# Moving a weight's mean-of-magnitudes pass ahead of the small-weight preparation in a fused layer on eight cores

## What is computed

```python
def _L0_attn_ref(x, Wa, ba, Wb, bb, Wout, bout):
    a = jnp.tanh(jnp.einsum('btd,sd->bts', x, Wa) + ba)
    b = jnp.tanh(jnp.einsum('btd,sd->bts', x, Wb) + bb)
    ...                      # scan over t: h = a_t * h + b_t, hs = all h
    return x + jnp.einsum('bts,ds->btd', hs, Wout) + bout

def _L0_ffn_ref(x, weight, bias):
    scale = jnp.mean(jnp.abs(weight))
    w_t = jnp.clip(jnp.round(weight / (scale + EPS)), -1.0, 1.0)
    w_ste = weight + jax.lax.stop_gradient(w_t * scale - weight)
    return jnp.einsum('bsi,oi->bso', x, w_ste) + bias

xn = _layernorm(x, axis=-1)
x = x + _L0_attn_ref(xn, ...) + _L0_ffn_ref(xn, ...)
```

## Time and profile before

| | us |
|---|---|
| median of 3 runs | 740.21 (740.07 to 740.62) |
| the profiled execution's own time | 739.39 |
| its span, slowest core (core 5) | 737.8 |
| fastest core (core 3) | 732.8 |
| PE busy | 590.1 (80% of the span) |
| DVE busy | 348.9 (47%) |
| ACT busy | 235.6 (32%) |
| POOL busy | 216.9 (29%) |

### The profile page before, as it was taken

One profiled execution on the slowest core, in us unless ns is written; L12 is line 12 of the kernel. 1 busy time (PEld: TensorE's weight loads), 2 busy tenths in 40 slices (PEclk: granted clock), 3 DMA queues, 4 the chain that ended last, 5 costly groups with the idle time before them and its releaser, 6 DMA issues.

```text
span 737.8 us, 11310 instructions; the slowest of 8 cores (732.8 to 737.8 us)
## 1 busy us (share of the span) xinstructions
PE 590.1 (80%) x3804; PEld 312.0 (42%) x3804; DVE 348.9 (47%) x303; ACT 235.6 (32%) x250; POOL 216.9 (29%) x742
## 2 busy tenths in 40 slices
PE   0121244425999999999999999999999999999995
PEld 0021234423444444454444444444444454454442
DVE  0000099983245564545555544445555545555521
ACT  1275434533223222223322223322222223322220
POOL 1000022354233333333334333333333333333310
PEclk9999999999999999999999999999999999999998
DMA  8979557801234333333333334333333333333322
GB/s 227 281 258 331 188 166 260 290 26 58 66 114 158 119 118 114 115 115 115 115 115 115 115 123 139 132 141 138 127 116 114 115 115 115 115 115 115 115 85 87
DMA packets 17071, 103.02 MB, mean 140 GB/s; under 512 B 4566, under 2 KB 4598, under 8 KB 4598
## 3 DMA queue, kind: packets, MB, share of 16 engines
q1 hardware_dynamic: 9590, 51.96, 22.2%
q0 software_dynamic: 7424, 50.34, 17.9%
HBM read 68.73 MB, written 33.55 MB: 139 GB/s over the span
## 4 chain that ended last, share of the span: by engine, by line
PE 66%; DMA 8%; ACT 8%; DVEq 4%; ACTq 4%; DVE 3%; issue 3%; SPq 2%; POOLq 1%; POOL 0%
PE pffn L513 15%; PE pffn L516 15%; PE pffn L528 15%; PE pffn L524 15%; ACT xnT L297 4%; DMA vv<-wf 4%; ACTq L296 3%; PE pab L501 3%; DVE wbn L345 2%; PE ptr L538 2%; DMA wasb<-wb 2%; DVEq L344 2%; SPq L171 2%; ACT xnT L293 1%; ACT xnT L232 1%
## 5 line engine op out<-in xcount | busy, mean ns | idle before, releaser
L513 PE MATMUL pffn<-w_rhs,xnT 128*128 128x512 bf16 x512 | 194.8, 380 | 0.0
L516 PE MATMUL pffn<-w_rhs,xnT 128*128 128x512 bf16 x512 | 194.6, 380 | 0.0
L524 PE MATMUL pffn<-w_rhs,xnT 128*128 128x512 bf16 x512 | 194.0, 379 | 0.0
L528 PE MATMUL pffn<-w_rhs,xnT 128*128 128x512 bf16 x512 | 194.0, 379 | 0.0
L357 DVE TENSOR_REDUCE sums<-sx 128x1 f32<-128x2048 f32 x32 | 73.1, 2286 | 148.7 <-DMA sx<-x 148.0
L293 ACT COPY xnT<-ptr 128x1024 bf16<-128x1024 bf16 x31 | 31.4, 1012 | 243.3 <-PE ptr L538 243.3
L275 ACT ACTIVATE xnb<-sx,nmr,yr 128x2048 bf16<-128x2048 f32 x31 | 64.9, 2094 | 102.2 <-POOLq L621 102.1
L391 DVE SCALAR_TENSOR_TENSOR outb<-pffn,negs,vv 128x1024 f32<-128x1024 f32 x32 | 41.1, 1284 | 114.7 <-PE pffn L554 114.7
L587 POOL TENSOR_SCALAR mm_<-sums 128x1 f32<-128x1 f32 x32 | 9.8, 307 | 241.1 <-DVE sqscr L359 232.8
L524 PEld LDWEIGHTS pffn<-w_rhs,xnT 128*128 128x128 bf16 x512 | 50.1, 98 | 60.4
L528 PEld LDWEIGHTS pffn<-w_rhs,xnT 128*128 128x128 bf16 x512 | 50.1, 98 | 60.4
(11 more groups left out here) (101 smaller groups left out, 583.2 us busy)
## 6 DMA issues: line engine op xcount, KB each, us to landing
sx<-x SPq DMA_DIRECT2D x32, 1024.0 KB, 5.5
y<-outb POOLq DMA_DIRECT2D x32, 1024.0 KB, 5.7
outb<-wf POOLq DMA_DIRECT2D x11, 1024.0 KB, 7.1
wtile<-wf SPq DMA_DIRECT2D x8, 1024.0 KB, 11.0
vv<-wf SPq DMA_DIRECT2D x8, 1024.0 KB, 10.9
sqscr<-wf POOLq DMA_DIRECT2D x5, 1024.0 KB, 6.6
wasb<-wa SPq DMA_DIRECT2D x1, 512.0 KB
wosb<-wout SPq DMA_DIRECT2D x16, 32.0 KB, 9.3
```

Of the source, the lines that this page charges most:

```text
L513: tensor.matmul(pffn[:, 0:512], lhs, w_rhs[:, 2048 * c:2048 * c + 512], start=st_, stop=False)
L516: tensor.matmul(pffn[:, 512:1024], lhs, w_rhs[:, 2048 * c + 512:2048 * c + 1024], start=st_, stop=False)
L524: tensor.matmul(pffn[:, 1024:1536], lhs, w_rhs[:, 2048 * c + 1024:2048 * c + 1536], start=st_, stop=False)
L528: ins = tensor.matmul(pffn[:, 1536:2048], lhs, w_rhs[:, 2048 * c + 1536:2048 * c + 2048], start=st_, stop=False)
```

## The change

Three queues are written in another order, and one group of transfers is merged.

- SP: the two tiles of x are loaded first, then the 16 tiles of `wf` for the magnitude pass with their waits, then the seven small tensors, then `Wout`, then (after `s_cast`) `Wb`. `Wout` is one transfer with a three-dimensional pattern in place of 16, so ACT's wait for it is on 16 and no longer on 256.
- ACT: the 16 absolute values come first, then all of stage 1.
- PE: the 256 matmuls of the magnitude pass come first. Ahead of them PE waits for a new semaphore `s_ms`, which DVE raises after its third memset (the column of ones they use), and no longer for `s_cvecv`. Then come the transposes of `Wa`, `Wb` and `Wout`, then the sum.
- DVE: a `drain` that raises `s_ms`. Its order is the same, so its wait for `s_small` still stands ahead of its wait for `s_pam`. POOL is not changed.

```diff
@@ sync
-            sync.dma_start(out=sidn[:, :], in_=idn_d[:, :]).then_inc(s_small, 16)
...
-            for j in range(NW):
-                sync.dma_start(out=wosb[:, 64 * j:64 * (j + 1)],
-                               in_=wo_d[128 * j:128 * (j + 1), :]
-                               ).then_inc(s_wol, 16)
             sync.dma_start(out=sx[:, 0:D], in_=x_d[0:TT, :]).then_inc(s_x0, 16)
...
+            sync.dma_start(
+                out=wosb[:, :].rearrange("p (j s) -> p j s", j=NW),
+                in_=wo_d[:, :].rearrange("(j p) s -> p j s", p=128)
+            ).then_inc(s_wol, 16)
+            sync.wait_ge(s_cast, 1)
+            sync.dma_start(out=wasb[:, :], in_=wb_d[:, :]).then_inc(s_wbl, 16)
@@ scalar
-            scalar.wait_ge(s_wol, 16 * NW)
+            scalar.wait_ge(s_wol, 16)
@@ vector
+            vector.drain().then_inc(s_ms, 1)
@@ tensor
+            tensor.wait_ge(s_ms, 1)
+            for j in range(NW):
+                tensor.wait_ge(s_wabs, j + 1)
...
-            tensor.wait_ge(s_cvecv, 1)
```

More of the change, by code:

```diff
@@ L116, in build @@
         s_pam = sem("s_pam")
+        s_ms = sem("s_ms")
         s_acp = sem("s_acp")
@@ L414, in _ @@
         def _(tensor):
+            tensor.wait_ge(s_ms, 1)
+            for j in range(NW):
+                tensor.wait_ge(s_wabs, j + 1)
+                for c in range(NCH):
+                    ins = tensor.matmul(
+                        spare[:, 0:1],
+                        xnT[:, (j % 2) * D + 128 * c:(j % 2) * D + 128 * (c + 1)],
+                        onescolb[:, :],
+                        start=(j == 0 and c == 0),
+                        stop=(j == NW - 1 and c == NCH - 1))
+                ins.then_inc(s_pam, 1)
             tensor.wait_ge(s_cast, 1)
```

46 lines of the change are left out of this document (17 added, 29 removed).

## The result

The changed kernel takes 741.93 us (median; 741.2 to 745.6), the kernel before on the same chip 739.74: a ratio of 1.0035 (95% interval 1.0024 to 1.0045), so about 2.6 us slower. The prediction was 738.9. Its range, 735.2 to 743.0, holds the time, but the time went the other way than forecast.

A forecast was written before the change was run, and what follows sets the result against it. Small work bounded the start, then large loads; behind the first ternary comparison lay a fixed 645.1 us. Loads ending 15.0 us earlier, less a tail of 21.2 where 7.5 stood, gave 1.3 us off the 740.21 median: 738.9, range 735.2 to 743.0.

The forecast's parts named there:

- the sum: Predicted start of DVE's first ternary comparison, 70.2 + 2.8 + 6.3 + 7.7 + 4.4 = 91.4 against 92.69: 1.3 us earlier.
- W: Landing of the last large tile, ahead of ACT's sixteenth absolute value: 70.2 us against 85.2 before, 15.0 earlier.
- to the cast of `Wa`: Small loads landing behind the last large tile, until ACT casts `Wa`: 2.8 us, between 1.6 and 4.
- to the cast of `Wb`: On ACT and SP: cast of `Wa` 1.9, issue 0.1, issue to landing of `Wb` 4.3: 6.3 us.
- to T: Cast of `Wb` to end of `Wout`'s transposes, 7.7 us, then from the sum's matmul to the first comparison, 4.4.
- T: Start of DVE's first comparison of the ternary pass: predicted 91.4 us against 92.69, its shift carried one to one to the end.
- Part 1: Large loads: 21 tiles of 1 MB in one unbroken stream at 3.15 us each, the last landing 15.0 us earlier.
- Part 2: Tail behind the last tile: small loads add 2.8 us, their issues nothing; `Wb` 6.3 us later; then stage 1 as today.
- The slower rival: `Wout`, queued ahead of `Wb` on SP, blocks it and delays the small loads: +1.9 us, 742.1, or 744.2; chance 0.20.
- Part 3: `Wout` as one transfer between small loads and `Wb` hides under other work; table load, DVE's wait and `s_ms` also 0.
- The faster one: Stream at 3.05 us a tile or better, small loads and `Wb` landing sooner: -4.6 us, 735.6; chance 0.25.
- The last, that the tail eats what the stream gains: Stream already bound by the DMA engines, so the tail takes back exactly its gain: 740.2, within a microsecond; chance 0.10.

The follow-up runs named there:

- experiment 14: Changed kernel with SP issuing the small loads only when the sixteenth large tile has landed: 743.96 us, ratio 1.0069 to the kernel before.
- experiments 13 and 14: 13: the changed kernel run once more as reference, 742.77 us; 14: the same with small loads waiting for the sixteenth tile, 743.96 us, on one chip.
- experiments 3 and 4: 3: changed kernel with `Wout` in 16 transfers again, 743.2 us; 4: kernel before with only `Wout` merged into one transfer, 740.74 us.
- experiment 2: Changed kernel with the transfer of `Wout` issued behind that of `Wb`: 743.04 us, ratio 1.0032 to the kernel before.
- experiment 1: Changed kernel with PE's matmul of the sum and the spread moved ahead of the transposes of `Wa`: 734.75 us, ratio 0.992 to the kernel before.

## Why the prediction was wrong

Two steps failed: the first term of the sum, W, which left out what is queued behind the last tile, and the comparison of the sum with the slowest core. The steps of the sum against core 6 of the changed kernel:

| step | predicted | measured | off |
|---|---|---|---|
| W, sixteenth absolute value | 70.2 | 72.52 | +2.3 |
| to the cast of `Wa` | 2.8 | 3.30 | +0.5 |
| to the cast of `Wb` | 6.3 | 7.10 | +0.8 |
| to T | 7.7 + 4.4 | 12.00 | -0.1 |
| T | 91.4 | 94.92 | +3.5 |

**What bounds.** Right. The change moved T and little else. From T to the end it is 645.4 us in the mean of the cores and 644.5 before, within the scatter of single cores (643.4 to 647.1 now); on core 6 it is 646.7 against the 645 predicted.

**Part 1, W: the step that failed.** With the queue behind the last tile empty W is 70.48 in the mean (experiment 14), where the sum says 70.2. What the sum left out is that eight transfers stand behind the last tile on its queue. With them there it lands 1.6 us later (experiments 13 and 14). That their bytes mix with the tile's is the likely way, but no view here shows single transfers. Part 2 said that the small loads' issues cost nothing because they are over in time; just for that reason they are in the queue while the tile is still under way. The slower rival let the runs of `Wout` mix into the small loads, but I never asked the same of the small loads and the tile. Of the 2.3 us, 1.6 are this, 0.3 is what even experiment 14 lies above 70.2, and 0.4 is core 6 and its run (the mean W is 72.18).

That the rest of this term is only 0.3 off is luck. At 340 GB/s a tile takes 3.08 us and not 3.15; with that the sum would give 68.7. So the start and the landing together took 5.8 us in experiment 14 and not the 3 + 1 of the sum, and the tiles, priced 1.5 too high in all, hid it.

**Part 2, small loads and `Wb`.** The term of 2.8 was 0.5 short. `Wb` landed 5.0 us after its issue where 4.3 was taken from the quiet main loop; its best window moves 197 GB/s. The idle time of ACT ahead of its cast is 2.91 us and not 4 to 5, only because 1.28 us of it now stand ahead of the copy to `wab`, which is done meanwhile; together they are 4.19. The chain from there to T came out to a tenth, as it was copied from the trace and nothing in it had changed.

**Part 3, `Wout`.** Right: zero, both ways (experiments 3 and 4). The table load, DVE's wait and `s_ms` also cost nothing.

**The comparison.** The sum used average prices, but was set against the T of the slowest core, 92.69, which lies 1.3 above the mean of the 8 cores, 91.37. Compared mean with mean the same sum gives no gain at all. That is the whole of the forecast gain, and the second step that failed. The mean T came out at 94.40, which is 3.0 above both the sum and the mean before. By terms, in the mean, these 3.0 are 2.0 in W, 0.6 up to the cast of `Wa`, 0.5 from there to the cast of `Wb`, and -0.1 behind it.

**The rivals.** The faster one is refuted: W and the small loads came in on the late side. The slower one has about the right time (742.1), but by luck: `Wout` does mix into the small loads, by about 1 us, yet it doesn't block `Wb`, and moving it changed nothing in T (experiment 2). The last, that the tail eats what the stream gains, is nearest in kind; the tail ate more.

**What the change overlooked** is shown by experiment 1: the sum needs nothing of stage 1, and stood behind it for 15 us. With the sum first the same load order is 0.8% faster than the kernel before, and with POOL's and x's tiles taken out of the stream and a shorter stage 1 the kernel is 2.7% faster.

## What to carry to other kernels

When loads are moved off the front of a queue, price them again at the place where they land: small loads behind the last large one delayed it and had nothing beside them, and in front or in the midst of the stream they cost about twice their bytes. Look at every engine's order for what is already complete and stands behind the moved work, as the sum did here; that was worth three times the whole effect of the change. Set a sum built of average durations against the mean of the cores, not against the slowest one.
